# A gather, cross and tower kernel: unit 1's loads held back, two one-hot tiles made by GpSimd, fewer filler transposes

## What is computed

```python
e = jnp.stack([tbl_0[ids[:, 0]], ..., tbl_23[ids[:, 23]]], axis=1)   # 1024 x 24 x 16
for W in (W0, W1, W2):                                               # three levels of 64 outputs
    Xk = jnp.einsum('bfd,bhd,fho->bod', X0, Xk, Wr)                  # X0 = e
    outs.append(Xk.sum(axis=2))
h = jnp.concatenate([z, dense_ctx], axis=1)
h = jnp.maximum(h @ W_top1 + b_top1, 0.0)
h = jnp.maximum(h @ W_top2 + b_top2, 0.0)
y = h @ W_top3
```

## Time and profile before

| | us |
|---|---|
| median of 3 runs | 372.42 |
| the three runs | 370.34, 372.42, 377.17 |
| the profiled execution's own time | 372.23 |
| its span in the trace | 370.4 |
| PE busy | 352.8 (95%) |
| DVE busy | 307.8 (83%) |
| POOL busy | 218.9 (59%) |

### The profile page before, as it was taken

How to read it: one execution, slowest core, us unless ns; L and a number is a source line. 1 busy time by engine, 2 the same in 40 slices (tenths; PEclk the granted TensorE clock), 3 DMA queues, 4 the chain that set the end, 5 groups by cost and what they waited for, 6 DMA issues and landing times.

```text
span 370.4 us, 7172 instructions
## 1 busy us (share of the span) xinstructions
PE 352.8 (95%) x2730; PEld 157.6 (43%) x2730; DVE 307.8 (83%) x309; ACT 191.3 (52%) x358; POOL 218.9 (59%) x332
## 2 busy tenths in 40 slices
PE   4977799999999999999999999999999999999997
PEld 1755323422433345534352454444343444344475
DVE  3993599789898999979898989898999989997600
ACT  2132124254343666665648476757375766645563
POOL 5888888888888888887873788888850000000000
PEclk9999999999999999999999999999999999999999
DMA  6459959959989699989999799979997999970000
GB/s 191 122 117 223 244 120 229 243 91 238 217 215 248 124 233 263 246 165 231 250 247 231 175 234 247 244 146 240 274 274 162 243 253 238 240 207 0 1 4 0
DMA packets 56918, 71.02 MB, mean 192 GB/s; under 512 B 31058, under 2 KB 35794, under 8 KB 56883
## 3 DMA queue, kind: packets, MB, share of 16 engines
q1 hardware_dynamic: 49428, 69.05, 77.9%
q0 software_dynamic: 5376, 1.39, 3.9%
q10 hardware_dynamic: 2080, 0.13, 0.4%
HBM read 49.04 MB, written 1.58 MB: 137 GB/s over the span
## 4 chain that ended last, share of the span: by engine, by line
PE 77%; DMA 12%; DVE 5%; ACT 3%; issue 2%; SPq 1%; DVEq 0%; ACTq 0%
PE ps_x L451 48%; PE ps_b L451 10%; PE ps_tower L451 9%; DMA B_sb<-x_sb 7%; PE ps_turn L451 6%; DVE Z L426 3%; DMA C<-x_scratch 3%; PE ps_turn L515 2%; PE ps_turn L523 1%; DMA small_ids_sb<-small_ids 1%; DVE Z L414 1%; ACT x_diag L757 1%; DMA x_scratch<-x_rows 1%; PE ps_tower L457 1%; ACT x_sb L745 0%
## 5 line engine op out<-in xcount | busy, mean ns | idle before, releaser
L426 DVE TENSOR_TENSOR Z<-A,ps_b 128x1024 f32<-128x1024 f32 x186 | 214.1, 1215 | 7.2 <-PE ps_b L451 4.0
L240 POOL DMA_INDIRECT x_rows<-tbl,ids_sb x168 | 178.8, 1064 | 55.0 <-POOL pause_sb L251 30.6
L451 PE MATMUL ps_x<-Z,w_sb 128*64 128x512 f32 x768 | 184.2, 598 | 0.7 <-DVE Z L426 0.5
L451 PEld LDWEIGHTS ps_x<-Z,w_sb 128*64 128x64 f32 x768 | 49.3, 136 | 78.7 <-issue 57.2
L414 DVE TENSOR_TENSOR Z<-A,C 128x1024 f32<-128x1024 f32 x48 | 57.7, 1222 | 24.9 <-PE ps_x L451 7.6
L757 ACT ACTIVATE x_diag<-ps_turn,mask_sb 128x192 f32<-128x192 f32 x128 | 50.7, 606 | 14.3 <-PE ps_turn L523 14.3
L451 PE MATMUL ps_x<-Z,w0s_sb 128*64 128x512 f32 x192 | 45.2, 597 | 2.5 <-DVE Z L414 2.3
L740 ACT COPY ps_b<-B_sb 128x1024 f32<-128x1024 f32 x36 | 37.0, 1028 | 10.2 <-DMA B_sb<-x_sb 9.9
L251 POOL MEMSET pause_sb<- 128x144 f32 x160 | 39.9, 249 | 0.1
L770 ACT COPY G<-ps_turn 128x416 f32<-128x416 f32 x31 | 15.7, 505 | 46.7 <-PE ps_turn L451 45.6
L451 PEld LDWEIGHTS ps_turn<-x_diag,x_rows 128*64 128x64 f32 x496 | 25.2, 137 | 17.7 <-issue 17.7
(11 more groups left out here) (72 smaller groups left out, 193.4 us busy)
## 6 DMA issues: line engine op xcount, KB each, us to landing
A<-x_scratch SPq DMA_DIRECT2D x48, 512.0 KB, 11.7
B_sb<-x_sb SPq DMA_DIRECT2D x72, 256.0 KB
C<-x_scratch SPq DMA_DIRECT2D x32, 512.0 KB, 4.9
x_rows<-tbl,ids_sb POOLq DMA_INDIRECT x168
x_quarters<-x_scratch SPq DMA_DIRECT2D x16, 96.0 KB
x_scratch<-x_rows SPq DMA_DIRECT2D x7, 192.0 KB, 4.6
small_sb<-x_sb SPq DMA_DIRECT2D x4, 256.0 KB, 8.2
w_sb<-w SPq DMA_DIRECT2D x2, 384.0 KB, 4.5
```

What stands on the lines that cost most here:

```text
L240: pool.indirect_dma_start(out=x0_rows[t % 2][:, f * D:(f + 1) * D], out_offset=None, in_=tables[f], in_offset=bass.IndirectOffsetOnAxis(ap ...
L426: nc.vector.tensor_tensor(Z[s % ZR][:, :], A[u % AS][i][:, :], B0_sb if u >= LB and j == 0 else ps_b[j % 2][:, :], ALU.mult)\
L451: return nc.tensor.matmul(out, lhsT, rhs, start=start, stop=stop)
```

## The change

Three things change. SyncE waits for C 1 of unit 0 to land before it issues unit 1's loads, and issues that unit's C ahead of its A. `WARM` goes from 16, 16, 16, 4 to 4, 4, 4, 4. The ones of the last two chunks of set 1 (chunks 8 and 9; the 17th and 18th of the 26 tiles of ones) are made by GpSimd, between its gathers of tile 0 and of tile 1, in the buffers of unit 1's A 0 and A 1; VectorE's ring of Z skips them.

```diff
-WARM = (16, 16, 16, 4)
+WARM = (4, 4, 4, 4)
+HOT_P = 2
+    P_AT = HOT.index((1, chunks[MADE[1][1]] - HOT_P))
+        pool_ones = [A[1][p] for p in range(HOT_P)]
+        def hot_ring(n):
+            return n if n < P_AT else n - HOT_P
@@ gpsimd
+            pool.wait_ge(ids_copied, 2)
+            pool.wait_ge(small_rows_in, 16)
+            for p in range(HOT_P):
+                c = HOT[P_AT + p][1]
+                nc.gpsimd.tensor_scalar(pool_ones[p][0:CR, :], small_ids_f32[1][0:CR, :], small_rows_sb[:, c:c + 1],
+                                        None, ALU.is_equal).then_inc(pool_hot_ready, 1)
             for t in range(1, TILES):
@@ sync
+            sp.wait_ge(C_in[0][1], 16)
+            for i in range(NI - 1):
+                load_c(1, i)
             for i in range(NI):
                 load_a(1, i)
-            for i in range(NI - 1):
-                load_c(1, i)
@@ vector
-                for c in range(chunks[MADE[m][1]]):
+                for c in range(chunks[MADE[m][1]] - (HOT_P if m == 1 else 0)):
@@ tensor
-                pe.wait_ge(hot_ready, n + 1)
+                if P_AT <= n < P_AT + HOT_P:
+                    pe.wait_ge(pool_hot_ready, n - P_AT + 1)
+                    ones = pool_ones[n - P_AT]
+                else:
+                    pe.wait_ge(hot_ready, hot_ring(n) + 1)
+                    ones = Z[hot_ring(n) % ZR]
```

More of the change, by code:

```diff
@@ L170, in cin_tower @@
         y_stored = sem("y_stored")
-        paused = sem("paused")
+        paused, pool_hot_ready = sem("paused"), sem("pool_hot_ready")
         ids_spread, hot_used, small_turned = sem("ids_spread"), sem("hot_used"), sem("small_turned")
@@ L383, in make_ones @@
                     dve.wait_ge(ids_copied, 2 * m)
-                for c in range(chunks[MADE[m][1]]):
-                    n = HOT.index((m, c))
-                    after(dve, hot_used, n - ZR + 1)
-                    nc.vector.tensor_scalar(Z[n % ZR][0:CR, :], small_ids_f32[m][0:CR, :], small_rows_sb[:, c:c + 1],
+                for c in range(chunks[MADE[m][1]] - (HOT_P if m == 1 else 0)):
+                    r = hot_ring(HOT.index((m, c)))
+                    if r >= ZR:
+                        used = r - ZR if r - ZR < P_AT else r - ZR + HOT_P
+                        dve.wait_ge(hot_used, used + 1)
+                    nc.vector.tensor_scalar(Z[r % ZR][0:CR, :], small_ids_f32[m][0:CR, :], small_rows_sb[:, c:c + 1],
                                             None, ALU.is_equal).then_inc(hot_ready, 1)
@@ L678, in _ @@
                               small_sb[:, SETS_AT[k] + c, f, :],
-                              Z[n % ZR][0:CR, TILE_ROWS * f:TILE_ROWS * (f + 1)], c == 0, c == chunks[k] - 1)
+                              ones[0:CR, TILE_ROWS * f:TILE_ROWS * (f + 1)], c == 0, c == chunks[k] - 1)
                 last.then_inc(hot_used, 1)
```

## The result

The changed kernel takes **379.36 us** (median of 15 runs, 375.71 to 381.05), against 374.24 us for the kernel before in the runs beside it (15 runs, 370.34 to 377.88). The ratio is **1.0144, 95% interval 1.0112 to 1.0177**: slower by 1.4%. The forecast was 372.9 us in a range of 369.5 to 378.0, so the time lies above the range, in the direction of the rival "GpSimd is far later". The profiled execution of the changed kernel took 380.35 us (span 378.6); the one of before, 372.23, was among that kernel's faster ones. The spans differ by 8.2 us, the medians by 5.1: the pair overstates the difference.

The account below looks back on a forecast made before the run. TensorE, 95% busy, was taken to bound the kernel, through when its body starts and what breaks in later. The body's 1.9 us gain is overtaken at unit 4 by GpSimd's 4.0 less 3.3 slack: 372.2 + 0.7 = 372.9 us, range 369.5 to 378.0.

Parts of the forecast that it names:

- GpSimd is far later: Rival: time ahead of tile 1's first gather delays tile 2's store and unit 4, one for one beyond 3.3 us; chance 0.22.
- GpSimd is 4.0 us later from there on: GpSimd after tile 1's first slow gathers: first pause 5.5 us later, less 1.5 us regained, leaves it 4.0 us late.
- Two tiles, 4.2 us: GpSimd's two tiles of ones: 1.64 us each scaled from the pause, plus 0.46 each waiting for VectorE, 4.2 for both.
- The extra instruction, 1.28 us: Instruction ahead of GpSimd's tiles, priced at 1.28 us like ScalarE's ACT_TABLE_LOAD in case it loads code.
- 1.5 us back from slow pauses: Tile 1's first gathers: about 2.5 of four slow pause-and-gather pairs beside VectorE's ones avoided, returning 1.5 us to GpSimd.
- later tiles have more room: Tiles behind unit 4: a tile takes some 40 us, its 24 gathers 35, so GpSimd's lateness should not matter there.
- The two tiles bring set 1's store nothing: Start of the kernel: VectorE free about 1.3 us sooner, but TensorE was held up 0.1 us at most, so the store stays.
- 0.6 sooner: Unit 0's C 1 lands 0.6 us sooner because unit 1's loads are held back; ends 0 and 2.5 us.
- What the hold costs: nothing lost: Unit 1's A 2 lands at 52.3, late by 0.3 us for VectorE's third product; TensorE doesn't feel it.
- TensorE's clock falls: Rival: with fewer fillers TensorE idles about 33 to 38 us, clock halves, body starts 1.9 us later, 374.1 us; chance 0.10.
- TensorE's time behind unit 4 is therefore the later of the two: From unit 4 on: the later of a 1.9 us sooner body start and 4.0 - 3.3 = +0.7 us decides.
- the gain is kept: Rival: GpSimd's tiles cost 1.0 us each, it is 1.4 later, within slack, so 370.3 us; chance 0.22.

Follow-up runs that it names:

- e17_spare: Kernel before plus two unused 128x1024 TENSOR_SCALARs on GpSimd ahead of tile 2's gathers: 378.73 us, ratio 1.0188.
- e16_fill: Changed kernel plus 56 filler transposes on TensorE ahead of unit 4's products: 378.8 us, ratio 1.0194 to the kernel before.
- e5_delay10: Kernel before plus ten waited pauses (MEMSETs of 128x144) on GpSimd ahead of tile 1's first gather: 379.67 us, ratio 1.0143.
- e8_no_pause: Changed kernel without the 40 pauses ahead of the gathers of tiles 1 and 2: 372.13 us, ratio 0.9947 to the kernel before.
- e15_no_pause: Changed kernel without the 40 pauses ahead of tiles 1 and 2's gathers, repeated on another chip: 372.1 us, ratio 1.0000 to the kernel before.
- e13_spare: Kernel before plus two unused 128x1024 TENSOR_SCALARs on GpSimd ahead of tile 2's gathers; one run in a slow group, the tiles took 4.92 and 2.85 us.
- e14: Kernel before without the 40 pauses ahead of the gathers of tiles 1 and 2: 370.7 us beside 371.27, ratio 0.9964.
- e7: Changed kernel with the tower's weights loaded behind unit 4's A and C instead of ahead: 378.83 us, ratio 1.0156 to the kernel before.
- e2: Kernel before with only WARM cut to 4, 4, 4, 4: 373.34 us, ratio 1.0023.
- e1: Kernel before with only unit 1's loads held until C 1 lands, its C ahead of its A: 375.58 us, ratio 1.0057.
- e4: Kernel before with hold and less warming, no ones on GpSimd: 374.1 us, ratio 1.0020.
- e6: Kernel before plus four waited pauses on GpSimd ahead of tile 1's first gather: 374.96 us, ratio 1.0054.

## Why the prediction was wrong

**The step that failed is a size: "GpSimd is 4.0 us later from there on".** It was 6.7 us at the first gather of tile 1, still 6.4 at the fifth, where 4.0 was meant to hold, and 9.9 at the 48th. By its terms:

- *Two tiles, 4.2 us.* They took 6.5. The price scaled from the pause by columns, 1.64 a tile, was too low by itself: 2.85 (e17_spare). The disturbance by VectorE that was added, 0.46 each, came out at 0.40 on average ((2.87 + 3.65) / 2 - 2.85).
- *The extra instruction, 1.28 us.* It took 0.04. The Trainium skill, "GPSIMD Engine Reference", section "Instruction dispatch", has a load of about 6 us at the first call of fresh code; here GpSimd's first tile began 0.1 us after that instruction and took no longer than the same operation in e17_spare, 2.87 to 2.85 us, so no such load shows. The two errors together are +2.3 - 1.24: the first pause came at 20.46 where 19.3 was forecast.
- *1.5 us back from slow pauses.* They didn't come: VectorE's ones lasted longer too, and the first two pauses were still slow, 0.76 and 0.64. Of the 1.5 only 0.3 had come back by the fifth gather (28.99 for 22.56).
- *Nothing more after that.* 3.5 us more came from the fifth gather of tile 1 to the last of tile 2 (the 48th of all). Of the 40 gathers of tiles 1 and 2 nine took over 1.2 us, five in the kernel before; the longest were 1.88 and 1.77. A long one runs beside VectorE's product of two SBUF tiles, as the rows of e16_fill show (1.97 and 1.64 beside L434, 0.95 else); which gathers meet one is chance of the schedule (one to nine in the other kernels' traces), so part of the 3.5 belongs to this pair of traces: in e16_fill, with the same program of GpSimd, the 48th gather was 5.2 us late, in the ones alone 7.1.

**The mechanism behind it was right.** SyncE lost another 1.4 us on its queue, so unit 4's C went out 11.5 us late; the prediction's 103.0 for the last A becomes 114.5, and VectorE began the third product at 114.71. Against the 106.3 at which it was needed that is 8.4 us, and the span is 8.2 longer. That this pair agrees so well is in part luck. In the ones alone, e5_delay10 and e17_spare the 48th gather was 7.1, 7.4 and 7.9 us late, for which the formula below gives 3.8, 4.1 and 4.6; unit 4 was 5.1, 5.2 and 5.7 us later than before, and the spans were 8.7, 7.1 and 8.1 longer. The place and the direction hold, the rate of one for one is too small: "later tiles have more room" doesn't cover what is lost behind unit 4. The rival "GpSimd is far later" named the place, the store and the rate of one for one; at 9.9 us of lateness its own formula, with 3.3 of slack, gives +6.6 on 372.2, 378.8 us, against a median of 379.36; between the medians, though, it is only 5.1. Its chance of 0.22 was too small, since the nearest row for an operation that reads was one that only writes. Ten pauses (e5_delay10) and the edit that takes the pauses away (e8_no_pause, e15_no_pause) show it from both sides.

**The ones.** "The two tiles bring set 1's store nothing" counted VectorE at 0.73 a tile. Four of its tiles took 1.5 to 2.0 us beside GpSimd's, and set 1's store went out 2.8 us later, not unchanged. It wasn't forecast, and it didn't show because C 1 then took 4.6 us, in the changed kernel and in the ones alone, which has no hold. C 0 and A 1 had been issued 3.9 us ahead of set 1's store there (23.33 for 27.20) and 0.2 behind it in the kernel before; that C 1 found them done is a reading, and no experiment tests it. The Trainium skill, "SBUF — State Buffer", section "SBUF: two separate sides", says that VectorE in its faster modes and GpSimd share a pair of ports under a lock held for the whole instruction, with the other blocked. That they collide the rows show, and that a VectorE product with one input in PSUM does not (e17_spare). A lock of whole instructions they don't: from 13.7 to 21.1 us VectorE made five tiles (the four slow ones and one of 0.74) and GpSimd its two, 7.4 us in all, where five of 0.74 and two of 2.85 one after the other are 9.4; and in e13_spare the product that began second was done at 50.3, before GpSimd's tile was, at 50.9. That the one that starts first keeps its time, as that page of the Trainium skill has it, those two tiles do show; the first pair of the changed kernel doesn't: VectorE's tile began at 13.7, ahead of GpSimd's at 14.0, and it was VectorE's that took 2.03 for 0.74, while GpSimd's took its 2.87.

**The hold.** "0.6 sooner" can't be seen, and the other answer, none, fits better: 5.7 us with it, 5.4 to 6.1 without where C 1 went out as late. The 0.6 MB that it was worked out from left out the 0.29 MB moved from 24.4 to 27 us, so it was too low by up to that. By the ring-order rule of the Trainium skill ("DMA: Bandwidth & Descriptors", section "Queues, rings and completion order") that the prediction cited it should give C 1 nothing; the runs agree with that. "What the hold costs: nothing lost" isn't refuted: alone it takes 375.58 us for 374.18, and its ratio shows no loss, as said above.

**Less warming.** The body starts 2.3 us sooner where 1.9 was forecast (40.54; the forecast said about 41), but that is luck: kernels with neither part start at 40.65 to 41.09 too, and what is sure of it is the third product's wait for the fillers, 0.6 us in the earlier trace rows (41.75 for 41.15), 2.0 with the hold alone and none in the changed kernel. The clock did fall near there in two kernels with less warming, from 35.8 to 39.3 us (less warming alone) and from 38.3 to 41.7 (with the hold); a product took 1.62 to 1.98 us there for 1.08. In the changed kernel it didn't. Falls at 24.7 to 25.4 us, ahead of everything that these parts change, stand in the traces with the hold, with both, and also in e17_spare, which has neither. So the rival "TensorE's clock falls" exists, costs up to 0.9 us a product there, and was not the cause.

**The gain wasn't to be kept anyway.** "TensorE's time behind unit 4 is therefore the later of the two" and "later tiles have more room" treat everything behind unit 4 as TensorE's. The kernels with hold or less warming alone pass unit 4 two us ahead of the trace of before and have lost it by unit 15; at unit 10 it is waits for A, and what takes the rest isn't isolated. Over the nine traces without the long stall at unit 4 the body's start says nothing of the span: with starts from 42.56 to 42.88 (before, e14, e7, e8) the spans are 370.4, 369.4, 373.5 and 373.4 us, with starts from 39.80 to 41.08 (e2, e1, e4, e15, e6) 371.0, 372.0, 371.6, 370.4 and 371.2. And hold and less warming together, with no ones on GpSimd, take 374.1 us beside 374.18. So the rival "the gain is kept" would have failed too, with no lateness of GpSimd at all.

## What to carry to other kernels

Before moving work to an engine that "has room", find which transfer hangs on its last instruction and count the slack from there: GpSimd was 59% busy on the page and had 3 us to give, since a store on SyncE's queue, the loads behind it and unit 4 hung on its 48th gather. Price an operation by a row that reads as well as writes on that engine, and keep the high end as the likely one where the nearest row does less. And check a head start further on: it is worth something only if the next resource (here the loads, at unit 10) isn't already just in time. Compare a start with that of several executions before calling it a gain: it was 42.88 us here and 41.09 in e17_spare, which has the same program up to there.

## What the runs showed of the hardware

- GpSimd's TENSOR_SCALAR on 128x1024 fp32 takes 2.85 us beside a VectorE product with one PSUM input, 2.87 and 3.65 us beside VectorE's TENSOR_SCALARs (themselves 0.74 to up to 2.03 us), and 4.92 us behind VectorE's products of two SBUF tiles.
- An indirect gather's issue on GpSimd takes 0.95 us, and 1.6 to 2.0 us when it meets VectorE's product of two SBUF tiles.
- In two groups of runs in which the kernel before took 410 and 419 us, three kernels with gathers issued without pauses had TensorE do 16 to 21 products and VectorE one tile from 20 to 32 us; kernels with the pauses in one of these groups did not, and neither did the same kernel on a chip of the common kind.
- TensorE's granted clock fell to 0.5 some 3 us after TensorE went idle at 103.7, and was back at 1.00 by 118, after it had worked again from 111.8.
